# Attention and mixture-of-experts block in fp32: where the softmax is divided by its sums

## The chip, the cores and the metric

The kernel runs on one core of one Trainium2 chip. The metric is the device time of one execution in microseconds (us). Engines are named as in the profile: PE is TensorE, PEld its weight loads, DVE is VectorE, ACT is ScalarE, POOL is GpSimd, SP is SyncE, whose queue issues most of the transfers.

## The reference, cut

64 blocks of 128 tokens: `x` is 64 x 128 x 256, the context 64 x 128 x 192. First a cross attention with 4 heads of 64, the keys being the 128 context rows and the block's own 128 rows:

```
xn, ln = layernorm(ctx), layernorm(layernorm(x))
q = ln @ Wq.T;  k, v = concat([xn @ Wkv.T, ln @ Wlkv.T])      # 256 keys
attn = softmax(where(mask, rmsnorm(q) * SCALE @ rmsnorm(k).T, -max))   # over the 256 keys
out = attn @ v                                                # by head
x = x + out @ Wo.T + bo
```

Then each token's normalised row goes to the 4 best of 32 experts (grouped top-k routing, gated feed-forward of width 128) and through a shared gated feed-forward of width 256; both are added to `x`. The change touches only `softmax` and `attn @ v`.

## The kernel before

All is fp32. The first stage, up to about 700 us, is attention and routing. It works through 32 units of two blocks each; a `Unit` `u` has blocks j = 0 and 1, and b = 2 * u.n + j counts blocks. The stage is software pipelined by hand: `in_order(step, UNITS)` runs `step(s)` for s = 0 to 31 on every engine, and each engine's `step` is a fixed order of calls that concern several units at a time: the attention of unit s, the projections of the next unit `a = s + 1`, the router of `cc = s - 2`, the slot assignment of `r = s - 3`, the input statistics of `run = s + 3` and `ahead = s + 4`. An engine runs its list strictly in that order, and semaphores (`wait_ge`, `then_inc`) join the lists. So the order of calls within a step decides what waits behind what. Steps 3 to 30 have all of these parts; steps 0 to 2 lack the router or the assignment, and step 31 has no next unit.

The attention of one block j of unit s goes as follows.

- PE `scores(s, j)` writes 4 heads x 128 queries x 256 keys into PSUM (`psS` for j = 0, `psT` for j = 1), line 813, with the mask, line 818.
- DVE `maxima(s, j)`, line 1460, takes the row maxima.
- ACT `exps(s, j)`, line 1160, writes `probs` in SBUF, one head at a time, and the row sums `den` (128 x 4).
- DVE `invert_sums(s, j)`, line 1466, makes `rden = 1 / den`, 128 x 4.
- ACT `weigh_probs(s, j)`, line 1168, multiplies the 4 heads of `probs`, 128 x 256 each, by `rden` in place.
- PE `turn_probs(s, j)`, line 827, transposes them in 8 pieces; ACT `probs_copy(s, j)`, line 1175, brings them back to SBUF.
- PE `mix_values(s, j)`, line 840, 16 matmuls into `psO[:, 0:256]`: the outputs come out turned, 64 rows of a head by 128 queries. ACT `o_copy(s, j)`, line 1182, copies them to `oT`.
- PE `out_proj(s, j)`, line 852; DVE `residual`, line 1473, adds the result to `x1`.

For the next unit DVE does `square_sums(a, j)` (line 1418), `norms` (a chain of small operations that ends at line 1448), `scale_heads(a, j)` (line 1454); then PE turns keys and queries (`turn_k`, lines 791 and 792, `turn_q`, line 800) and ACT copies them (`k_copy`, line 1200, `q_copy`, line 1206). `scores` of the next step needs `q_copy`. In DVE's step the router's operations follow: `best_groups`, then `best_experts` and `choose_experts` (from line 1506).

DVE's order within a full step: `maxima(s,0)`, reading the ranks and assigning, `invert_sums(s,0)`, `maxima(s,1)`, rest of the assignment and `top_scores(cc)`, `invert_sums(s,1)`, `square_sums` twice, `norms`, `scale_heads` twice, `best_groups`, `best_experts`, `choose_experts`.

PE's order: `scores(s,0)`, turning and positions for the router, `scores(s,1)`, logits, the projections of `a` (lines 757, 767, 770), `turn_probs(s,0)`, `project_v` (line 778) twice, `turn_c`, `mix_values(s,0)`, `turn_x`, `turn_probs(s,1)`, `out_proj(s,0)`, `turn_k(a,0)`, `mix_values(s,1)`, `turn_k(a,1)`, `turn_q(a)`, `out_proj(s,1)`.

After the attention come the first part of the shared feed-forward, the expert tiles (about 749 to 1190 us), and the rest of the shared part with the sums. POOL scatters the routed rows during the attention stage, paced by PE's semaphores.

Of the kernel before, what the change touches and what calls it, by code (L numbers as in the profile page):

```python
# [17 lines left out]
P = 128  # L18
NB, D, DC = 64, 256, 192
H, DH = 4, 64  # L20
# [66 lines left out]
def build(nc, x, ctx, mask, gains, w_in_lat, w_in_ctx, wo, bo,  # L87
# [8 lines left out]
    with ExitStack() as c:  # L96
# [45 lines left out]
        probsT = part(2, 2, H * P)  # L142
        oT = part(D)
        vv = part(4 * 2, H, DH)

# [27 lines left out]
        nmax = sb("nmax", [P, 2, H])  # L173
        den, rden = sb("den", [P, 2, H]), sb("rden", [P, 2, H])

# [63 lines left out]
        s_full, m_done, exp_done = sem("s_full"), sem("m_done"), sem("exp_done")  # L239
        den_done, rden_done = sem("den_done"), sem("rden_done")  # L240
        spread = [sem("spread0"), sem("spread1")]
        pt_full, pt_ev = sem("pt_full"), sem("pt_ev")
        pv_full, ot_ev = sem("pv_full"), sem("ot_ev")
        y_full, y_done = sem("y_full"), sem("y_done")
# [465 lines left out]
        def _(pe):  # L710
# [111 lines left out]
            def turn_probs(u, j):  # L822
# [6 lines left out]
                m.then_inc(pt_full, 1)  # L829

            def mix_values(u, j):
                b = 2 * u.n + j
                pe.wait_ge(pt_ev, b + 1)
                pe.wait_ge(pc_free, 2 * u.n + 2)
                ge(pe, ot_ev, b)
                for ch in range(2):
                    for key in range(2):
                        for r in range(2):
                            g, h = 2 * r + ch, 2 * ch + r
                            m = pe.matmul(psO[r * DH:(r + 1) * DH, ch * P:(ch + 1) * P],  # L840
                                          vv[:, 4 * u.par + 2 * j + key, h, :], probsT[:, j, key, g * P:(g + 1) * P],
                                          start=key == 0, stop=key == 1)
                m.then_inc(pv_full, 1)
# [87 lines left out]
            def step(s):  # L931
# [12 lines left out]
                if a.exists():  # L944
                    project_q(a, 0)
                    project_kv(a)
                    project_q(a, 1)
                turn_probs(s, 0)
                if a.exists():
                    project_v(a, 0)  # L950
                    project_v(a, 1)
# [5 lines left out]
                turn_probs(s, 1)  # L957
                out_proj(s, 0)
                if a.exists():
                    turn_k(a, 0)  # L960
# [121 lines left out]
        def _(act):  # L1082
# [72 lines left out]
            def exps(u, j):  # L1155
                b = 2 * u.n + j
                act.wait_ge(m_done, b + 1)
                ge(act, pt_full, b - 1)
                for g in range(H):
                    a = act.activation(probs[:, j, g, :], score_banks[j][:, g // 2, g % 2], ACT.Exp,  # L1160
                                       bias=nmax[:, j, g:g + 1], accum_out=den[:, j, g:g + 1])
                a.then_inc(den_done, 1)

            def weigh_probs(u, j):
                b = 2 * u.n + j
                act.wait_ge(rden_done, b + 1)
                for g in range(H):
                    a = act.activation(probs[:, j, g, :], probs[:, j, g, :], ACT.Copy, scale=rden[:, j, g:g + 1])  # L1168
                a.then_inc(exp_done, 1)
# [7 lines left out]

            def o_copy(u, j):
                b = 2 * u.n + j
                act.wait_ge(pv_full, b + 1)  # L1180
                ge(act, y_full, b)
                act.activation(oT, psO[:, 0:D], ACT.Copy).then_inc(ot_ev, 1)

# [25 lines left out]
            def step(s):  # L1209
# [9 lines left out]
                if cc.exists():  # L1219
                    logit_exp(cc)  # L1220
                weigh_probs(s, 0)
                if a.exists():
                    projected_q(a, 0)
                exps(s, 1)
                if a.exists():
                    projected_kv(a, 0)
                    projected_kv(a, 1)
                    projected_q(a, 1)
                probs_copy(s, 0)
                if a.exists():  # L1230
                    values_copy(a, 0)
                    values_copy(a, 1)
                weigh_probs(s, 1)
                o_copy(s, 0)
                if (s + 2).exists():
                    inputs_x(s + 2)
                probs_copy(s, 1)
                if (s + 2).exists():
                    inputs_c(s + 2)
                if a.exists():  # L1240
                    k_copy(a, 0)
                o_copy(s, 1)
                if a.exists():
# [120 lines left out]
        def _(dve):  # L1364
# [98 lines left out]
            def invert_sums(u, j):  # L1463
                b = 2 * u.n + j
                dve.wait_ge(den_done, b + 1)
                dve.reciprocal(rden[:, j, :], den[:, j, :]).then_inc(rden_done, 1)  # L1466

# [180 lines left out]
            def step(s):  # L1648
# [30 lines left out]

                def between_choices(n):  # L1680
                    if ahead.exists() and G_LINKS < n <= G_LINKS + 4:
                        input_part(ahead, n - G_LINKS - 1)
# [19 lines left out]
                if a.exists():  # L1702
                    square_sums(a, 0)
                    square_sums(a, 1)
                norms(run, between_roots if a.exists() else None)
                if a.exists():
                    scale_heads(a, 0)
                    scale_heads(a, 1)
                    if r.exists():
                        give_slots(r)  # L1710
# [4 lines left out]
                if not cc.exists() or not a.exists():  # L1715
                    residual(s, 0)
                    x1_statistics(s, 0)
                if not cc.exists():
                    if ahead.exists():
                        input_statistics(ahead)  # L1720
# [248 lines left out]
```

## Time and profile before

| | before |
|---|---|
| runs | 1341.43, 1343.05, 1344.83 us (median 1343.05) |
| profiled execution | 1343.46 us, its span 1341.5 us |
| granted TensorE clock, mean | 0.985 |
| busy share of the span | PE 97%, PEld 78%, DVE 72%, ACT 75%, POOL 48% |
| busy in 45 to 700 us (655 us) | PE 641.7, DVE 566.8, ACT 614.9, POOL 329.1 us |
| busy in 780 to 1110 us (330 us) | PE 330.0, DVE 177.9, ACT 230.1, POOL 210.1 us |

The second part of the table reads per stage: in the attention stage three engines are over 85% busy, in the expert stage only PE is full. The span is what the profiler saw from the first to the last instruction; the execution's own time is 1.96 us longer.

### The profile page before, as it was taken

Reading aid. Unit: us, or ns where it says so; the run is one execution under the profiler, and the core shown is the slowest. Engines: PE = TensorE matmul, PEld = TensorE weight load, DVE = VectorE, ACT = ScalarE, POOL = GpSimd, SP = SyncE. Lnnn points to the kernel's source line nnn. Section 1 sums busy time; section 2 is a strip of 40 time slices with the busy share of each in tenths; the row PEclk is TensorE's granted clock in tenths of the full one; section 3 lists DMA queues with packets and bytes.
Section 4 is the critical chain, followed back from the end, with each engine's and each line's share of the span. In section 5 each row is a group of like instructions: output and inputs, shape, how many; then the busy total and the mean of one; then the engine's idle time right before and its main releaser. Section 6 shows DMA issues by size and latency. Waiting matters only on the chain.

```text
span 1341.5 us, 32944 instructions
## 1 busy us (share of the span) xinstructions
PE 1298.0 (97%) x8718; PEld 1043.2 (78%) x8718; DVE 972.0 (72%) x4498; ACT 1011.6 (75%) x2730; POOL 643.4 (48%) x724
## 2 busy tenths in 40 slices
PE   6999999999999999999979899999999999999997
PEld 4566676676676766766658799999999999988886
DVE  4578898888988988888887455555555555548887
ACT  4899999999999999999851566766776676653332
POOL 1113555555555555555455366666666666640000
PEclk8999999999999999999989899999999999999999
DMA  8234645535545445454487655555655555438896
GB/s 278 84 133 136 205 162 176 192 131 187 176 138 190 161 153 195 136 179 162 168 304 246 194 169 172 172 172 168 178 169 174 169 173 166 132 114 313 304 319 218
DMA packets 147714, 247.14 MB, mean 184 GB/s; under 512 B 24139, under 2 KB 110413, under 8 KB 146896
## 3 DMA queue, kind: packets, MB, share of 16 engines
q1 hardware_dynamic: 121472, 177.63, 41.3%
q0 software_dynamic: 26064, 67.42, 14.5%
q8 instruction: 77, 1.26, 0.4%
q14 instruction: 101, 0.83, 0.2%
HBM read 104.68 MB, written 119.96 MB: 167 GB/s over the span
## 4 chain that ended last, share of the span: by engine, by line
PE 63%; ACT 21%; DVE 9%; issue 5%; DMA 2%; SPq 0%; POOL 0%; ACTq 0%; DVEq 0%
PE psT L1033 10%; PE ps L1033 9%; PE psS L1043 9%; ACT arena L1168 6%; PE ps L916 6%; PE ps L1024 5%; PE ps L852 4%; ACT arena L1160 4%; PE psS L927 3%; PE psT L827 3%; PE psS L813 3%; PE psO L840 2%; ACT arena L1128 2%; ACT arena L1132 2%; ACT arena L1175 2%
## 5 line engine op out<-in xcount | busy, mean ns | idle before, releaser
L701 POOL DMA_INDIRECT expert_out<-pay,dest x287 | 282.1, 983 | 175.1 <-DVE dest L1878 157.4
L556 POOL DMA_INDIRECT lists<-pay,slot x168 | 174.3, 1037 | 187.7 <-PE psT L827 39.6
L1043 PE MATMUL psS<-arena,history 128*128 x574 | 171.8, 381 | 0.3 <-DVE history L1865 0.3
L1033 PEld LDWEIGHTS ps<-pad,hist_j 128*128 128x128 f32 x1152 | 152.1, 193 | 9.5 <-ACT pad L1315 2.1
L1033 PEld LDWEIGHTS psT<-pad 128*128 128x128 f32 x1144 | 151.0, 192 | 7.3
L1033 PE MATMUL ps<-pad,hist_j 128*128 128x128 f32 x1152 | 152.8, 276 | 1.9 <-ACT pad L1315 1.9
L1033 PE MATMUL psT<-pad 128*128 128x128 f32 x1144 | 151.6, 276 | 0.0
L1872 DVE TENSOR_SCALAR pay<-psS,dest 128x256 f32<-128x256 f32 x287 | 138.9, 484 | 1.6 <-PE psS L1043 1.5
L757 PE MATMUL ps<-arena 128*128 128x512 f32 x256 | 128.3, 624 | 2.6 <-ACT arena L1120 2.0
L556 POOL DMA_INDIRECT lists<-arena,slot x88 | 91.0, 1034 | 79.4 <-PE psT L827 20.6
L1168 ACT ACTIVATE arena<-arena,rden 128x256 f32<-128x256 f32 x256 | 109.1, 503 | 15.2 <-DVE rden L1466 15.1
L1865 DVE TENSOR_TENSOR history<-history,psT 128x128 f32<-128x128 f32 x143 | 41.2, 288 | 102.4 <-ACT history L1326 102.4
L1865 DVE TENSOR_TENSOR history<-history,ps 128x128 f32<-128x128 f32 x144 | 41.5, 288 | 101.2 <-ACT history L1326 101.2
L1024 PE MATMUL ps<-ident,pay 128*128 128x128 f32 x574 | 110.0, 274 | 3.1 <-DMA arena<-in_gate_up 3.0
L1315 ACT ACTIVATE pad<-ps 128x256 f32<-128x256 f32 x287 | 107.7, 375 | 0.0
L1320 ACT ACTIVATE hist_j<-arena 128x512 f32 x144 | 89.6, 622 | 9.4 <-issue 7.6
L1326 ACT ACTIVATE history<-ps 128x128 f32<-128x128 f32 x144 | 39.9, 277 | 70.3 <-PE ps L1033 70.3
L757 PEld LDWEIGHTS ps<-arena 128*128 128x128 f32 x256 | 44.2, 193 | 59.2 <-issue 59.2
L1320 ACT ACTIVATE pad<-arena 128x512 f32 x143 | 88.8, 621 | 0.0
L1326 ACT ACTIVATE history<-psT 128x128 f32<-128x128 f32 x143 | 39.7, 278 | 65.0 <-PE psT L1033 65.0
L1043 PEld LDWEIGHTS psS<-arena,history 128*128 128x128 f32 x574 | 86.9, 192 | 0.7 <-issue 0.7
L1418 DVE TENSOR_REDUCE va<-arena 128x12 f32<-128x768 f32 x64 | 61.0, 953 | 34.2 <-ACT arena L1128 29.1
(238 smaller groups left out, 3284.1 us busy)
## 6 DMA issues: line engine op xcount, KB each, us to landing
lists<-pad SPq DMA_DIRECT2D x72, 516.0 KB, 5.2
pay<-lists SPq DMA_DIRECT2D x287, 129.0 KB, 2.2
arena<-expert_out SPq DMA_DIRECT2D x32, 1024.0 KB, 7.1
pay<-pay SPq DMA_DIRECT2D x42, 384.0 KB, 3.6
x<-in_x SPq DMA_DIRECT2D x32, 256.0 KB, 4.7
out<-arena SPq DMA_DIRECT2D x31, 256.0 KB, 5.8
arena<-arena SPq DMA_DIRECT2D x20, 384.0 KB, 3.4
arena<-in_ctx SPq DMA_DIRECT2D x32, 192.0 KB, 4.6
```

The lines of the kernel that those rows point to most:

```text
L556: pool.indirect_dma_start(lists, bass.IndirectOffsetOnAxis(ap=slots(u)[:, j, k:k + 1], axis=0), paid(u)[:, j, k, :], None).then_inc(scat[3 ...
L701: pool.indirect_dma_start(expert_out, bass.IndirectOffsetOnAxis(ap=dest[:, t % DESTS, 1:2], axis=0), yy[n], None, bounds_check=T * TOPK - ...
L757: m = pe.matmul(ps[0][:, :], lnT[:, k, tok], w_lat[:, k, 0:2 * D], start=k == 0, stop=k == 1)
L916: m = pe.matmul(up_banks[u % 2][mm][:, which * D:(which + 1) * D], w[:, k, mm * P:(mm + 1) * P], n1T_of(u)[:, k, :], start=k == 0, stop=k ...
L1024: m = pe.transpose(ps[n % 2][:, k * P:(k + 1) * P], xs[n][:, k * P:(k + 1) * P], ident[:, :])
L1033: m = pe.matmul(ps[2 + n % 2][:, which * P:(which + 1) * P], w_now[1 - n % 2][:, k, which * I:(which + 1) * I], xsT[:, n % 2, k * P:(k + 1 ...
L1043: pe.matmul(dbank[n % 2][:, 0:D], hh[:, n % 4, :], w_dn[:, at(e, 1), :].rearrange("p a n -> p (a n)"), start=True, stop=True)\
L1168: a = act.activation(probs[:, j, g, :], probs[:, j, g, :], ACT.Copy, scale=rden[:, j, g:g + 1])
L1315: act.activation(xsT[:, n % 2, :], ps[n % 2][:, 0:D], ACT.Copy).then_inc(xst_ev, 1)
L1320: act.activation(w_now[1 - n % 2], w_gu[:, at(e, 1)].rearrange("p a k n -> p (a k) n"), ACT.Copy)\
L1865: dve.tensor_tensor(hh[:, n % 4, :], sg[:, n % 4, :], ps[2 + n % 2][:, P:2 * P], ALU.mult)\
L1872: dve.tensor_scalar(yy[n], dbank[n % 2][:, 0:D], dest[:, t % DESTS, 0:1].bitcast(fp32), None, ALU.mult)\
```

## The change

`exps` now signals `exp_done` itself, and `turn_probs` turns the undivided exponentials. `invert_sums` writes the inverse sums wide, 128 x 256: each head's inverse 64 times side by side, in the order of the output rows. PE's new `turn_sums` transposes this in two 128 x 128 pieces into `psO[:, 256:512]`, ACT's `sums_copy` (in place of `o_copy`) brings it to SBUF as `wide_sums`, and DVE's new `divide` multiplies `psO[:, 0:256]` by it into `oT`. `weigh_probs` and `o_copy` are gone. `divide(s, 0)` stands on DVE after `norms`, `divide(s, 1)` in the middle of `best_experts`.

```diff
--- before.py
+++ after.py
@@ -141,6 +141,8 @@
         probs = part(2, H, 2 * P)
         probsT = part(2, 2, H * P)
         oT = part(D)
+        wide_sums = part(D)
+        rden = part(2, D)
         vv = part(4 * 2, H, DH)
 
         pay_mid = part(2, TOPK, ROW)
@@ -171,7 +173,7 @@
         va, ra, nb = sb("va", [P, 30]), sb("ra", [P, 30]), sb("nb", [P, 6])
         ry, rt = sb("ry", [P, 30]), sb("rt", [P, 30])
         nmax = sb("nmax", [P, 2, H])
-        den, rden = sb("den", [P, 2, H]), sb("rden", [P, 2, H])
+        den = sb("den", [P, 2, H])
 
         esc = sb("esc", [P, 2, E])
         sc = sb("sc", [P, 2, E])
@@ -237,9 +239,10 @@
         pa_free, pb_free, pc_free = sem("pa_free"), sem("pb_free"), sem("pc_free")
         sq_full, ss_done, scaled = sem("sq_full"), sem("ss_done"), [sem("scaled0"), sem("scaled1")]
         s_full, m_done, exp_done = sem("s_full"), sem("m_done"), sem("exp_done")
-        den_done, rden_done = sem("den_done"), sem("rden_done")
+        rden_done = sem("rden_done")
         spread = [sem("spread0"), sem("spread1")]
         pt_full, pt_ev = sem("pt_full"), sem("pt_ev")
+        sums_turned, sums_ev = sem("sums_turned"), sem("sums_ev")
         pv_full, ot_ev = sem("pv_full"), sem("ot_ev")
         y_full, y_done = sem("y_full"), sem("y_done")
         pay_x, lg_full, lg_exp = sem("pay_x"), sem("lg_full"), sem("lg_exp")
@@ -828,11 +831,19 @@
                                          probs[:, j, g, key * P:(key + 1) * P], ident[:, :])
                 m.then_inc(pt_full, 1)
 
+            def turn_sums(u, j):
+                b = 2 * u.n + j
+                pe.wait_ge(rden_done, b + 1)
+                ge(pe, ot_ev, b)
+                for ch in range(2):
+                    m = pe.transpose(psO[:, D + ch * P:D + (ch + 1) * P], rden[:, j, ch * P:(ch + 1) * P], ident[:, :])
+                m.then_inc(sums_turned, 1)
+
             def mix_values(u, j):
                 b = 2 * u.n + j
                 pe.wait_ge(pt_ev, b + 1)
                 pe.wait_ge(pc_free, 2 * u.n + 2)
-                ge(pe, ot_ev, b)
+                pe.wait_ge(sums_ev, b + 1)
                 for ch in range(2):
                     for key in range(2):
                         for r in range(2):
@@ -946,6 +957,7 @@
                     project_kv(a)
                     project_q(a, 1)
                 turn_probs(s, 0)
+                turn_sums(s, 0)
                 if a.exists():
                     project_v(a, 0)
                     project_v(a, 1)
@@ -956,6 +968,7 @@
                     turn_x(s + 2)
                 turn_probs(s, 1)
                 out_proj(s, 0)
+                turn_sums(s, 1)
                 if a.exists():
                     turn_k(a, 0)
                 mix_values(s, 1)
@@ -1156,16 +1169,10 @@
                 b = 2 * u.n + j
                 act.wait_ge(m_done, b + 1)
                 ge(act, pt_full, b - 1)
+                ge(act, rden_done, b - 1)
                 for g in range(H):
                     a = act.activation(probs[:, j, g, :], score_banks[j][:, g // 2, g % 2], ACT.Exp,
                                        bias=nmax[:, j, g:g + 1], accum_out=den[:, j, g:g + 1])
-                a.then_inc(den_done, 1)
-
-            def weigh_probs(u, j):
-                b = 2 * u.n + j
-                act.wait_ge(rden_done, b + 1)
-                for g in range(H):
-                    a = act.activation(probs[:, j, g, :], probs[:, j, g, :], ACT.Copy, scale=rden[:, j, g:g + 1])
                 a.then_inc(exp_done, 1)
 
             def probs_copy(u, j):
@@ -1175,11 +1182,11 @@
                 act.activation(probsT[:, j].rearrange("p k n -> p (k n)"),
                                score_banks[j][:, :, :, :].rearrange("p k a n -> p (k a n)"), ACT.Copy).then_inc(pt_ev, 1)
 
-            def o_copy(u, j):
+            def sums_copy(u, j):
                 b = 2 * u.n + j
-                act.wait_ge(pv_full, b + 1)
-                ge(act, y_full, b)
-                act.activation(oT, psO[:, 0:D], ACT.Copy).then_inc(ot_ev, 1)
+                act.wait_ge(sums_turned, b + 1)
+                ge(act, ot_ev, b)
+                act.activation(wide_sums, psO[:, D:2 * D], ACT.Copy).then_inc(sums_ev, 1)
 
             def n1_copy(u):
                 act.wait_ge(t_n, u.n + 1)
@@ -1218,7 +1225,6 @@
                 exps(s, 0)
                 if cc.exists():
                     logit_exp(cc)
-                weigh_probs(s, 0)
                 if a.exists():
                     projected_q(a, 0)
                 exps(s, 1)
@@ -1227,19 +1233,18 @@
                     projected_kv(a, 1)
                     projected_q(a, 1)
                 probs_copy(s, 0)
+                sums_copy(s, 0)
                 if a.exists():
                     values_copy(a, 0)
                     values_copy(a, 1)
-                weigh_probs(s, 1)
-                o_copy(s, 0)
                 if (s + 2).exists():
                     inputs_x(s + 2)
                 probs_copy(s, 1)
+                sums_copy(s, 1)
                 if (s + 2).exists():
                     inputs_c(s + 2)
                 if a.exists():
                     k_copy(a, 0)
-                o_copy(s, 1)
                 if a.exists():
                     k_copy(a, 1)
                     q_copy(a)
@@ -1462,8 +1467,18 @@
 
             def invert_sums(u, j):
                 b = 2 * u.n + j
-                dve.wait_ge(den_done, b + 1)
-                dve.reciprocal(rden[:, j, :], den[:, j, :]).then_inc(rden_done, 1)
+                dve.wait_ge(exp_done, b + 1)
+                ge(dve, sums_turned, b - 1)
+                dve.reciprocal(rden[:, j, :].rearrange("p (c r d) -> p c r d", c=2, r=2),
+                               den[:, j, :].rearrange("p (r c o) -> p c r o", c=2, o=1).to_broadcast([P, 2, 2, DH]))\
+                   .then_inc(rden_done, 1)
+
+            def divide(u, j):
+                b = 2 * u.n + j
+                dve.wait_ge(pv_full, b + 1)
+                dve.wait_ge(sums_ev, b + 1)
+                ge(dve, y_full, b)
+                dve.tensor_tensor(oT, psO[:, 0:D], wide_sums, ALU.mult).then_inc(ot_ev, 1)
 
             def residual(u, j):
                 b = 2 * u.n + j
@@ -1678,6 +1693,8 @@
                         x1_statistics(s, 0)
 
                 def between_choices(n):
+                    if n == G_LINKS + 1:
+                        divide(s, 1)
                     if ahead.exists() and G_LINKS < n <= G_LINKS + 4:
                         input_part(ahead, n - G_LINKS - 1)
 
@@ -1703,6 +1720,7 @@
                     square_sums(a, 0)
                     square_sums(a, 1)
                 norms(run, between_roots if a.exists() else None)
+                divide(s, 0)
                 if a.exists():
                     scale_heads(a, 0)
                     scale_heads(a, 1)
@@ -1716,6 +1734,7 @@
                     residual(s, 0)
                     x1_statistics(s, 0)
                 if not cc.exists():
+                    divide(s, 1)
                     if ahead.exists():
                         input_statistics(ahead)
 
```

## Rows read from the trace of the kernel before

**Rows 1.** Windows view, one step: start:end, length, busy PE, PEld, DVE, ACT, POOL; clock, DMA.
```profile
320.78:341.37 20.59, 20.46 (x138) 13.94 (x139) 18.36 (x106) 19.90 (x55) 11.27 (x13) 1.00 0.50 167
```

**Rows 2.** Starts of `maxima(s, 0)`, VectorE: start, us, engine, line, form, idle before.
```profile
94.30 1.22 DVE L1460 TENSOR_REDUCE nmax<-psS 128x4 f32<-128x1024 f32 x1 [0.60 <-PE psS L818]
...
320.78 1.23 DVE L1460 TENSOR_REDUCE nmax<-psS 128x4 f32<-128x1024 f32 x1 [0.52 <-PE psS L818]
...
341.37 1.22 DVE L1460 TENSOR_REDUCE nmax<-psS 128x4 f32<-128x1024 f32 x1 [0.53 <-PE psS L818]
...
670.77 1.22 DVE L1460 TENSOR_REDUCE nmax<-psS 128x4 f32<-128x1024 f32 x1 [1.25 <-PE psS L818]
```

**Rows 3.** The same step on VectorE in order of time.
```profile
324.40 0.18 DVE L1466 RECIPROCAL rden<-den 128x4 f32<-128x4 f32 x1
...
329.20 0.18 DVE L1466 RECIPROCAL rden<-den 128x4 f32<-128x4 f32 x1 [0.40 <-ACT arena L1160]
...
331.26 0.95 DVE L1418 TENSOR_REDUCE va<-arena 128x12 f32<-128x768 f32 x1 [0.90 <-ACT arena L1128]
...
334.99 1.83 DVE L1454 TENSOR_TENSOR arena<-arena,ra 128x768 f32<-128x768 f32 x2
...
338.29 0.29 DVE L1506 TENSOR_TENSOR t<-sfc,gm 128x32 f32<-128x32 f32 x2
```

**Rows 4.** VectorE costs by line (min/median/max ns), and one group of the lines view.
```profile
L1480 DVE RECIPROCAL sc<-esc x32: 543/544/553, 78.9 to 703.6; 128x64 f32<-128x64 f32 x32
...
L1553 DVE RECIPROCAL wsum<-wsum x31: 165/166/167, 96.9 to 716.5; 128x2 f32<-128x2 f32 x31
...
L1473 DVE TENSOR_TENSOR x<-x,ps x64: 395/414/422, 49.1 to 691.7; 128x256 f32<-128x256 f32 x64
...
L1570 DVE TENSOR_TENSOR code<-code,later 128x64 f32<-128x64 f32 x27 | 6.1, 225 | 0.9
```

**Rows 5.** The same step on ScalarE in order of time.
```profile
324.61 1.70 ACT L1168 ACTIVATE arena<-arena,rden 128x256 f32<-128x256 f32 x4 [0.53 <-DVE rden L1466]
...
333.06 1.69 ACT L1168 ACTIVATE arena<-arena,rden 128x256 f32<-128x256 f32 x4
...
338.36 0.41 ACT L1182 ACTIVATE arena<-psO 128x256 f32<-128x256 f32 x1
...
338.86 0.60 ACT L1200 ACTIVATE arena<-ps 128x512 f32<-128x512 f32 x1
...
339.35 0.68 ACT L1206 ACTIVATE arena<-ps,gain 128x512 f32<-128x512 f32 x1
```

**Rows 6.** The same step on TensorE in order of time.
```profile
335.74 1.03 PE L852 MATMUL ps<-arena 128*128 128x256 f32 x4
...
336.61 0.27 PE L791 MATMUL ps<-ident,arena 128*128 128x128 f32 x1
...
337.14 1.09 PE L840 MATMUL psO<-arena 128*64 128x128 f32 x16
...
338.16 0.33 PE L791 MATMUL ps<-ident,arena 128*128 128x128 f32 x1
...
338.65 0.62 PE L800 MATMUL ps<-ident,arena 128*128 128x128 f32 x4
...
340.08 1.13 PE L813 MATMUL psS<-arena 64*128 64x256 f32 x8
```

**Rows 7.** Waits of TensorE weight loads in 100 to 650 us: sum, times, longest.
```profile
PEld psT L827 <- ACT arena L1168: 9.9, 27, 0.4
...
PEld psS L813 <- ACT arena L1206: 9.4, 27, 0.4
```

**Rows 8.** TensorE clock before the last step: windows, then two timeline rows.
```profile
670.00:673.00 3.00, 0.73 (x8) 0.30 (x5) 1.22 (x1) 0.83 (x2) 1.93 (x2) 1.00 0.40 155
...
676.00:680.00 4.00, 4.00 (x17) 3.36 (x14) 3.75 (x20) 2.20 (x8) 0.97 (x1) 0.50 1.13 388
...
674.06 2.08 PE L813 MATMUL psT<-arena 64*128 64x256 f32 x8
```

## The prediction

> **What bounds the kernel now.** I read the page first, then the windows view to see which stage the change touches. It touches the attention stage alone, the first 700 us. There one step is a cycle of 20.59 us in which PE is busy for 20.46, ACT for 19.90 and DVE for 18.36 [rows 1]. The starts of `maxima(s, 0)` give the step more exactly: from step 3 to step 31 they go from 94.30 to 670.77 us, 28 steps of 20.59 us [rows 2]. All else was read from the timeline of one of them, the one from 320.78 to 341.37.
>
> PE and ACT are both nearly full. DVE, which gets the new work, looks like the one with room, and its room is what the argument turns on. It waits visibly three times in a step: 0.53 us for the scores [rows 2], 0.40 us for the second sums and 0.90 us for a projected square [rows 3]. That is 1.83 us. The other 20.59 - 1.83 = 18.76 us are work and the small gaps between dependent operations, and they stay.
>
> **The change part by part.** *ACT loses `weigh_probs`.* Two groups of four take 1.70 and 1.69 us, and the wait of 0.53 us for the inverse in front of the first goes too [rows 5]. `sums_copy` costs what `o_copy` cost, the same 128x256 from the same PSUM tile, 0.41 us. So ACT's step falls by 3.4 us of work to about 16.5 us busy. Time comes of this only if ACT was what the step waits for and nothing else takes its place.
>
> *PE gains `turn_sums`*, two 128x128 transposes for each block, four in a step. The four of `turn_k(a, 1)` take 338.65 - 338.16 = 0.49 us [rows 6], so PE needs at most 20.46 + 0.49 = 20.95 us. Of that up to 0.7 us is a wait for ACT that the busy row can hide: 9.9 and 9.4 us over 27 steps in front of the second `turn_probs` and of `scores` [rows 7]. PE thus wants between 20.2 and 20.95 us: as much as the step now has.
>
> *DVE's `invert_sums` goes from 4 to 256 elements a row.* This is the price that decides, and the trace has no reciprocal of this size. It has three smaller ones: 2 elements 166 ns, 4 elements 180 ns [rows 3, 4], 64 elements 544 ns [rows 4]. From 4 to 64 that is 6.1 ns an element, against 1.0 ns for a plain tensor operation (225 ns for 64 elements, 414 ns for 256) [rows 4]. A reciprocal is thus paid by the element. Estimate: 180 + 252 x 6.1 = 1717 ns, 1.54 us more than now, twice a step: 3.08 us. Bounds: from below, all beyond 64 elements at the plain rate, 544 + 192 x 1.0 = 740 ns, that is 2 x 0.56 us; from above, everything proportional, 4 x 544 = 2180 ns, 2 x 2.0 us. I take 1.72 us, since the small ones show a fixed part (2 elements cost as much as 92% of 4) and a slope that no plain operation has.
>
> The Trainium skill ("VectorE: DVE Perf Modes", First, the fixed hardware budget) says that the reciprocal is an iterative divide with a repeat count of 8 on an engine of 0.96 GHz. If that count is taken as cycles per element it is 8.3 ns, an estimate of 2.13 us for 256 elements; it would put the sum below near the upper bound. The rows give 6.1 ns, so they agree on the kind of cost and not on its size.
>
> *DVE gains `divide`*, twice a step. The nearest row is `residual`, a 128x256 tensor operation of SBUF and PSUM, 0.41 us [rows 4]. Operations overlap by some 0.08 us at their ends, so 0.33 us each, 0.66 us in a step.
>
> *The sum on DVE*: 18.76 + 3.08 + 0.66 = 22.50 us, against a step of 20.59. DVE's 1.83 us of waiting are spent and 1.91 us are missing. DVE becomes the engine that sets the step.
>
> *The new waits.* `divide(s, 0)` stands behind `norms`, and PE holds `out_proj(s, 0)`, `turn_sums(s, 1)`, `turn_k(a, 0)`, `mix_values(s, 1)`, `turn_k(a, 1)` and `turn_q` in line behind it. So the second limit is a loop. `norms` ends and `scale_heads` begins now 14.21 us after `maxima(s, 0)` [rows 2, 3]; without the waits of 0.40 and 0.90 us and with both reciprocals that is 12.91 + 3.08 = 15.99 us. `divide` lands at 16.40. `out_proj` starts at about 16.5 and takes 336.61 - 335.74 = 0.87 us; `turn_sums` lands 0.38 us later, at 17.75; `sums_copy` 0.41 us, to 18.16; `mix_values` from 18.26 takes 338.16 - 337.14 = 1.02 us; `turn_k` 0.49 us, to 19.77; `turn_q` lands 0.62 us later [rows 5, 6], at 20.39. ACT can begin `q_copy` then, `k_copy` being 0.49 us ahead of it; from the start of `q_copy` to the next `maxima` it is 341.37 - 339.35 = 2.02 us [rows 2, 5]. The loop closes at 22.4 us. It lies 0.1 us under DVE's own sum, so the two limits will now and then hold each other up, and I take 22.6 us. `divide(s, 1)` comes due on DVE at about 19.7 (338.29 is 3.30 us behind the start of `scale_heads` [rows 3]), when `mix_values(s, 1)` has just landed; it holds `out_proj(s, 1)`, which PE reaches at 20.3, so it costs nothing more.
>
> The moved signals cost nothing: the exponentials of a block are ready before DVE comes to invert their sums (0.40 us late now in the second case, early after, as DVE itself comes 1.5 us later), and `turn_probs` stands behind projections that PE has to do first. POOL's scatters and SP's transfers follow PE's semaphores, POOL is busy 11.27 of 20.59 us [rows 1], and a longer step gives them room.
>
> *The total*: 28 full steps x (22.6 - 20.59) = 56 us. Steps 0 to 2 lack the router's share of DVE's work and hide the new work. The last step and the way out of the stage get one reciprocal and one `divide` on their path, 1.54 + 0.41 = 2 us. 1343.46 + 58 = 1402 us for an execution like the profiled one, which lies 0.4 us over the median of the runs; I say 1402.
>
> **The rivals.** *The reciprocal is dearer than its slope*: at 2.18 us DVE's sum is 23.4 and the loop 23.3 us, so 23.5 for the step, 28 x 2.9 + 2.5 = 84 us, 1427 us. The 8-fold repeat would do about this. Against it: 64 elements at 8.3 ns would leave 0.01 us for all else in an operation of 0.544 us, and 2 elements already take 0.166 us [rows 4].
>
> *The wait at `out_proj(s, 0)` is longer than drawn*, by ACT's fixed order (`sums_copy(s, 1)` behind `probs_copy(s, 1)`) or landings that I put too short. One microsecond more in the loop gives 23.4 us a step, 1425 us. For it: the loop has some seven hand-overs from one engine to another. Against it: ACT is 6 us idle in such a step.
>
> *TensorE's clock falls.* Ahead of the last step PE did 0.73 us of work in 3 us, and then ran at granted clock 0.50, 1.2 GHz instead of 2.4; eight score matmuls took 2.08 us [rows 8], against 1.13 us at full clock [rows 6]. If the new gap in front of `out_proj(s, 0)`, about 1.5 us, did this in each step, some 2.5 us would go each time, on the loop: 1402 + 70 = 1472 us. Against it: PE still is busy some 20.5 of 22.6 us.
>
> *No difference*: the wide reciprocal costs only its extra elements at the plain rate, 0.74 us. DVE's sum is 18.76 + 1.12 + 0.66 = 20.54 us, PE sets the step at 20.6 to 20.7, 1343 to 1347 us.
>
> *Faster*: ACT was holding PE. With ACT 3.4 us lighter PE's waits of 0.7 us go, PE gains 0.49, and the step is 20.59 - 0.7 + 0.49 = 20.38 us: 28 x 0.21 = 6 us, 1337 us. It needs a sum on DVE no longer than that: 18.76 + 0.66 + two increments of at most 0.48, so a wide reciprocal of at most 0.18 + 0.48 = 0.66 us, hardly above the 0.544 us that a quarter of it takes. From that point on the added work decides.
>
> **How the numbers follow.** The likeliest, 1.72 us for the reciprocal with DVE's sum as the limit: 0.75, with a range of its own of 1390 to 1418 (step 22.2 to 23.2). Dearer reciprocal 0.07, longer loop 0.06, clock 0.04, no difference 0.04, faster 0.04. The range reaches down past the likeliest by a few microseconds for a cheaper reciprocal and up to the first two rivals, 1385 to 1430. A measurement of this kernel tells 0.3%, 4 us, from nothing: faster 0.04, same 0.04, slower 0.92.
>
> **What would show it.** In the timeline after: RECIPROCAL 128x256 at about 1.7 us; starts of `maxima(s, 0)` 22.6 us apart; DVE busy for over 21.5 us of a step and its waits for ACT gone; ACT idle for 5 to 6 us, PE waiting for DVE ahead of `out_proj(s, 0)`, at an unchanged clock; the stages after 700 us moved as a block. The prediction is wrong if the reciprocal comes under 0.8 us, or if PE's wait at `out_proj(s, 0)` spreads to more than about 2 us.

## The result and the profile after

The changed kernel takes 1403.6 us in the median of 4 runs (1402.6 to 1404.5) against 1343.9 us for the kernel before; the ratio is 1.0445, 95% interval 1.0424 to 1.0465. The profiled execution took 1403.49 us with a span of 1401.5 us, at the same mean granted clock of 0.985.

The windows view over one step of the changed kernel, to be held against [rows 1] (start:end, length, busy PE, PEld, DVE, ACT, POOL, clock, DMA share, GB/s):

```profile
323.38:345.95 22.57, 21.05 (x142) 14.46 (x143) 21.98 (x108) 17.01 (x48) 11.59 (x13) 1.00 0.45 152
```

DVE went from 18.36 to 21.98 us busy and is the fullest engine; ACT fell from 19.90 to 17.01; PE rose from 20.46 to 21.05 at full clock. The starts of `maxima(s, 0)`, as in [rows 2], for steps 3, 4 and 31 (timeline of DVE):

```profile
97.84 1.23 DVE L1465 TENSOR_REDUCE nmax<-psS 128x4 f32<-128x1024 f32 x1 [0.37 <-PE psS L821]
120.26 1.23 DVE L1465 TENSOR_REDUCE nmax<-psS 128x4 f32<-128x1024 f32 x1
...
729.06 1.22 DVE L1465 TENSOR_REDUCE nmax<-psS 128x4 f32<-128x1024 f32 x1 [0.93 <-PE psS L821]
```

28 steps take 631.22 us, 22.54 each, against 20.59. That is 54.7 us of the 60.0 by which the span grew. The row at 120.26 has no bracket any more: the view names no idle time of DVE ahead of it. The rest: from `maxima(31, 0)` to the end 672.4 us instead of 670.7, 1.7 us; steps 0 to 2 together 61.68 instead of 60.80 us, 0.9 us; and the first `maxima` comes at 36.16 instead of 33.50 us, 2.7 us.

The new and changed groups of DVE (lines view, 100 to 650 us: count, then busy us and mean ns, then idle before), and the step on DVE and PE in order of time (timeline views):

```profile
L1472 DVE RECIPROCAL arena<-den 128x256 f32<-128x256 f32 x50 | 87.7, 1753 | 1.7
...
L1481 DVE TENSOR_TENSOR arena<-psO,arena 128x256 f32<-128x256 f32 x48 | 20.2, 421 | 0.8
```

```profile
332.96 1.75 DVE L1472 RECIPROCAL arena<-den 128x256 f32<-128x256 f32 x1
...
339.28 0.42 DVE L1481 TENSOR_TENSOR arena<-psO,arena 128x256 f32<-128x256 f32 x1
...
343.13 0.42 DVE L1481 TENSOR_TENSOR arena<-psO,arena 128x256 f32<-128x256 f32 x1
...
345.63 0.17 DVE L1543 TENSOR_TENSOR before<-before,chosen 128x32 bf16<-128x32 bf16 x1
```

```profile
333.44 0.38 PE L839 MATMUL psO<-ident,arena 128*128 128x128 f32 x2
...
339.76 1.13 PE L863 MATMUL ps<-arena 128*128 128x256 f32 x4 [1.40 <-DVE arena L1481]
...
341.28 0.27 PE L795 MATMUL ps<-ident,arena 128*128 128x128 f32 x1
341.68 1.09 PE L851 MATMUL psO<-arena 128*64 128x128 f32 x16
...
345.63 0.28 PE L821 MATMUL psS<-mask_row,ones_sq 64*128 64x256 bf16 x2
```

The divisions start 15.90 and 19.75 us behind `maxima(s, 0)` at 323.38; the prediction had 15.99 and 19.7. PE stands 1.40 us ahead of `out_proj(s, 0)` (line 863) until `divide(s, 0)` is done, and a smaller hold is seen between the last turned key at 341.28 and `mix_values(s, 1)` at 341.68, which waits for the copy of the turned sums.

The last row of each view shows how the step closes. By the ends that the profile gives, DVE's last operation ends at 345.63 + 0.17 = 345.80 us, PE's last mask matmul of the next scores at 345.63 + 0.28 = 345.91, and the next `maxima(s, 0)` starts at 345.95. So DVE does wait, for 0.14 us, too short for the view to name; nearly every full step has this gap, 0.13 to 0.15 us. DVE's own work, with the small gaps inside it, takes 22.43 us of the step, and the loop through PE closes last by 0.14 us.

### The profile page after: what moved, and what is told of

It reads as the page before. It is cut to its first block, busy times and chain, and to the rows that moved or that the text cites. A ratio compares the mean times of both kernels' runs of the same rounds, so it can differ in the third digit from the quotient of the medians.

```text
span 1401.5 us, 33170 instructions
## 1 busy us (share of the span) xinstructions
PE 1316.2 (94%) x8846; PEld 1060.6 (76%) x8846; DVE 1086.0 (77%) x4562; ACT 918.8 (66%) x2474; POOL 650.1 (46%) x724
## 4 chain that ended last, share of the span: by engine, by line
PE 59%; DVE 30%; issue 7%; ACT 2%; DMA 1%; SPq 0%; ACTq 0%; DVEq 0%; POOL 0%
PE ps L1046 9%; PE psT L1046 9%; PE psS L1056 9%; PE ps L927 5%; PE ps L863 5%; PE ps L1037 4%; DVE nmax L1465 4%; DVE arena L1472 4%; DVE va L1423 3%; PE psS L938 3%; PE psO L851 3%; DVE arena L1604 3%; PE psS L816 3%; PE psT L927 2%; PE ps L794 1%
## 5 line engine op out<-in xcount | busy, mean ns | idle before, releaser
L559 POOL DMA_INDIRECT lists<-pay,slot x168 | 166.3, 990 | 213.6 <-PE ps L773 32.6
L559 POOL DMA_INDIRECT lists<-arena,slot x88 | 87.0, 989 | 102.5 <-PE psT L830 16.6
L1472 DVE RECIPROCAL arena<-den 128x256 f32<-128x256 f32 x64 | 112.2, 1753 | 9.7 <-ACT arena L1174 7.7
L863 PE MATMUL ps<-arena 128*128 128x256 f32 x256 | 70.8, 400 | 42.5 <-DVE arena L1481 42.4
L549 POOL TENSOR_TENSOR x<-x,bo_b 128x512 f32<-128x512 f32 x32 | 40.7, 1273 | 95.2 <-PE psS L821 95.2
```

The lines of the kernel that those rows point to most:

```text
L559: pool.indirect_dma_start(lists, bass.IndirectOffsetOnAxis(ap=slots(u)[:, j, k:k + 1], axis=0), paid(u)[:, j, k, :], None).then_inc(scat[3 ...
L863: m = pe.matmul(ps[1][:, 0:D], oT[:, k * P:(k + 1) * P], w_o[:, k, :], start=k == 0, stop=k == 1)
L1472: dve.reciprocal(rden[:, j, :].rearrange("p (c r d) -> p c r d", c=2, r=2), den[:, j, :].rearrange("p (r c o) -> p c r o", c=2, o=1).to_br ...
```

## The experiments

The theory: DVE's own work sets the step, mostly by the wide reciprocal (A). The rival: the new hand-overs through `divide`, the turned sums and their copies set it, whatever DVE's load (B). A third question came up on the way: what PE's four new transposes (0.44 us a step) cost, and what ACT's relief is worth.

| kernel | time, before beside it (us) | ratio, 95% interval | step (us) |
|---|---|---|---|
| before | 1343.9 | 1 | 20.59 |
| changed | 1403.6 | 1.0445 (1.0424 to 1.0465) | 22.54 |
| e1, spare wide reciprocal | 1377.6 / 1344.3 | 1.0252 (1.0235 to 1.0269) | 21.78 |
| e2, narrow, PE widens | 1380.0 / 1344.3 | 1.0258 (1.0240 to 1.0276) | 21.80 |
| e3, narrow, ACT widens | 1380.4 / 1344.3 | 1.0264 (1.0247 to 1.0282) | 21.68 |
| e4, divide late | 1490.2 / 1344.3 | 1.1078 (1.1058 to 1.1098) | 25.46 |
| e5, divide early | 1405.6 / 1343.8 | 1.0457 (1.0439 to 1.0476) | 22.55 |
| e6, no weighing | 1331.6 / 1343.8 | 0.9912 (0.9894 to 0.9930) | 20.23 |
| e7, widened in ACT's gaps | 1357.4 / 1343.8 | 1.0101 (1.0083 to 1.0120) | 21.01 |
| e8, sums together | 1357.9 / 1343.8 | 1.0101 (1.0083 to 1.0119) | 21.02 |
| e9, spare turns | 1420.3 / 1406.7 | 1.0097 (1.0079 to 1.0115) | 21.15 |
| e10, copy for reciprocal | 1413.2 / 1406.7 | 1.0043 (1.0029 to 1.0057) | 20.98 |
| e11, divide first | 1416.3 / 1406.7 | 1.0085 (1.0067 to 1.0104) | 20.79 |
| e12, one block | 1350.7 / 1344.8 | 1.0037 (1.0022 to 1.0051) | 20.88 |

The step is the distance of the starts of `maxima(3, 0)` and `maxima(31, 0)` in each trace, over 28. In some traces this mean holds a few longer steps, whose cause was not looked for: most steps are 20.89 us in e7 and e10, 21.02 in e9 and 20.80 in e12.

Runs e9 to e11 were made on another chip, on which the kernel before took 1406.7 us; their times are read only as ratios to that. The extra 60 us lie behind the attention stage: from `maxima(31, 0)` to the end of the span it is 730 to 735 us in e9 to e11, against 671 in the kernel before. Their steps are compared with 20.59 us, though no trace shows the step of the kernel before on that chip. The traced execution of e10 took 1417.0 us and is the slowest of its five.

**e1: the reciprocal alone.** The kernel before with

```diff
                 dve.reciprocal(rden[:, j, :], den[:, j, :]).then_inc(rden_done, 1)
+                dve.reciprocal(spare[:, j, :].rearrange("p (c r d) -> p c r d", c=2, r=2),
+                               den[:, j, :].rearrange("p (r c o) -> p c r o", c=2, o=1).to_broadcast([P, 2, 2, DH]))
```

> The kernel before, with the wide reciprocal added on DVE behind the narrow one; nothing reads its result, and no other part of the change is made. Theory A (DVE's time is what the change costs): DVE's occupied 18.8 us of a step grow by 2 x 1.67 to 22.1, the step goes from 20.6 to 22.1 to 22.6, the time to 1387 to 1401. Rival B (the new hand-overs through divide, turned sums and their copy cost the time): nothing of them is here, so the step stays at 20.6 to 20.9 and the time at 1344 to 1352.

It took 1377.6 us, ratio 1.0252: more than half of the whole loss with none of the hand-overs. Its windows view of one step and the group of the reciprocal (lines view):

```profile
312.69:334.48 21.79, 20.68 (x138) 13.88 (x139) 21.38 (x109) 20.25 (x55) 11.00 (x13) 1.00 0.47 157
```

```profile
L1468 DVE RECIPROCAL arena<-den 128x256 f32<-128x256 f32 x52 | 89.5, 1722 | 0.0
```

DVE is busy for 21.38 of 21.79 us. The step is 0.3 us under the 22.1 of the expectation, so the 18.8 us that I had taken as fixed contained about 0.3 us that a fuller DVE does not need. Rival B gave at most 20.9 and falls as the sole cause. DVE's last operation ends here as the next `maxima` begins: the gap of 0.14 us is absent.

**e2 and e3: narrow sums.** The changed kernel with the narrow reciprocal, and the widening given to PE (e2) or to ACT, in two copies ahead of `probs_copy` (e3):

```diff
-                dve.reciprocal(rden[:, j, :].rearrange("p (c r d) -> p c r d", c=2, r=2),
-                               den[:, j, :].rearrange("p (r c o) -> p c r o", c=2, o=1).to_broadcast([P, 2, 2, DH]))\
-                   .then_inc(rden_done, 1)
+                dve.reciprocal(rden4[:, j, :], den[:, j, :]).then_inc(rden_done, 1)
...
+                    for r in range(2):                                            # e2, for each ch
+                        m = pe.matmul(psO[r * DH:(r + 1) * DH, D + ch * P:D + (ch + 1) * P],
+                                      rden4[:, j, 2 * r + ch:2 * r + ch + 1].to_broadcast([P, DH]), ident[:, :],
+                                      start=True, stop=True)
...
+                act.activation(rden[:, j, :].rearrange("p (c r d) -> p c r d", c=2, r=2),   # e3, widen(u, j)
+                               rden4[:, j, :].rearrange("p (r c o) -> p c r o", c=2, o=1).to_broadcast([P, 2, 2, DH]),
+                               ACT.Copy).then_inc(widened, 1)
```

> The changed kernel with the inverse sums kept narrow (128x4, 0.18 us); PE widens them while it turns them, by four 64-column matmuls on a repeated column per block. Theory A: DVE's occupied time falls to 19.2 to 19.5 us, PE is next with at most 20.9, the step is 20.4 to 20.9 and the time 1338 to 1352. Rival B: the hand-overs are all still here, so the step stays near 22 us and the time over 1385.

> The changed kernel with narrow inverse sums that ACT, which is idle for 5.5 us of a step, copies wide (two copies of some 0.4 us in a step). Theory A: DVE 19.2 to 19.5, PE at most 20.9, step 20.4 to 20.9, time 1338 to 1352. If ACT's order is what matters, one more copy ahead of probs_copy delays mix_values, and this is slower than the version where PE widens. Rival B: over 1385.

Both missed: 1380 us, a step of 21.8 and 21.7. With 3.1 us a step of reciprocals taken off DVE only 0.8 came back. The traces say why, each in its own way. In e2 (windows view of a step, then PE's widening matmuls in the timeline):

```profile
317.96:339.79 21.83, 21.83 (x154) 14.76 (x155) 19.03 (x107) 17.21 (x47) 11.25 (x13) 1.00 0.46 156
```

```profile
328.13 0.66 PE L839 MATMUL psO<-ident,rden 128*64 128x128 f32 x8
```

DVE is down to 19.03 us, and PE has no idle time at all in 21.83. My four matmuls are eight records, 328.13 to 328.72 us in the timeline, 0.6 us a block, where the two transposes of the changed kernel are two records, the next operation starting 0.22 us behind them: in the traces an fp32 matmul leaves two records and an fp32 transpose one. (The 16 matmuls of `mix_values` and the eight of `scores` named ahead of the result are records as well; the kernel issues 8 and 4.) The 0.38 us more for each block, twice a step, on top of PE's 21.0 us give the step of 21.8. In e3 PE waits instead (waits view, 100 to 650 us: sum, times, longest):

```profile
PE psO L840 <- ACT arena L1190: 15.1, 25, 0.6
```

That is 0.6 us a step at `turn_sums(s, 0)` for ACT's widening, which I had put too late in ACT's order.

**e4 and e5: the place of `divide(s, 0)`.** The same work, `divide(s, 0)` behind both `scale_heads` (e4), or in the middle of `norms` (e5):

```diff
-                divide(s, 0)
                 if a.exists():
                     scale_heads(a, 0)
                     scale_heads(a, 1)
+                divide(s, 0)                     # e4
...
+                    if n == 6:                   # e5, in between_roots
+                        divide(s, 0)
```

> The changed kernel with divide(s, 0) moved behind both scale_heads on DVE: the same work on every engine. If the loop over PE (out_proj, turned sums, copy, mix, turns of keys and queries, scores) is a limit as tight as DVE's sum, it grows by 1.74 us, the step to 24.3 and the time to 1452. If DVE's sum alone sets the step, it stays at 22.5 and the time at 1403.

> The changed kernel with divide(s, 0) moved forward on DVE, into the middle of norms (behind its sixth operation), some 1.5 us earlier; the same work on every engine. In the changed kernel the loop over PE and DVE's own sum close within 0.2 us of each other at 22.5 us. If DVE's sum is a limit of its own, taking 1.5 us out of the loop brings nothing: step 22.4 to 22.6, time 1399 to 1405. If the loop alone sets the step, it falls to PE's own need of 21.1 us, time 1365.

e5 took 1405.6 us, a step of 22.55: unchanged. In the timeline of DVE `divide(s, 0)` now stands at 14.53 us behind `maxima` instead of 15.90, and the next `maxima` again follows DVE's last operation by 0.14 us. PE's wait has gone from `out_proj(s, 0)` to `turn_k(a, 0)`, which waits for `scale_heads`, and 0.27 us of it to `out_proj(s, 1)`, which waits for `divide(s, 1)` (timeline of DVE, then of PE):

```profile
324.37 1.23 DVE L1465 TENSOR_REDUCE nmax<-psS 128x4 f32<-128x1024 f32 x1
...
338.90 0.42 DVE L1481 TENSOR_TENSOR arena<-psO,arena 128x256 f32<-128x256 f32 x1
...
346.95 1.22 DVE L1465 TENSOR_REDUCE nmax<-psS 128x4 f32<-128x1024 f32 x1
```

```profile
341.64 0.33 PE L794 MATMUL ps<-ident,arena 128*128 128x128 f32 x1 [0.91 <-DVE arena L1459]
344.61 1.13 PE L863 MATMUL ps<-arena 128*128 128x256 f32 x4 [0.27 <-DVE arena L1481]
```

So DVE's sum is a limit of its own: whatever is taken out of the loop, no more than 0.14 us a step can come back. e4 shows that the loop is one too, and dearer than I expected: 1490.2 us, a step of 25.46 instead of 24.3. Two rows of PE's timeline, from step 5 and from step 11, and two windows, the whole of step 5 and the gap in step 11, have the reason:

```profile
169.06 1.13 PE L863 MATMUL ps<-arena 128*128 128x256 f32 x4 [3.13 <-DVE arena L1481]
...
321.19 2.07 PE L863 MATMUL ps<-arena 128*128 128x256 f32 x4 [3.13 <-DVE arena L1481]
```

```profile
150.94:175.21 24.27, 21.01 (x142) 14.43 (x143) 22.16 (x107) 16.95 (x47) 11.22 (x13) 1.00 0.45 152
...
318.00:324.00 6.00, 2.87 (x10) 2.33 (x10) 3.88 (x20) 1.43 (x3) 2.68 (x3) 0.73 0.12 43
```

PE now stands for 3.0 to 3.1 us in front of `out_proj(s, 0)` in every step. In steps 3 to 5 the clock stays at 1.00, `out_proj` takes its 1.13 us, and the steps are 24.13, 24.27 and 24.27 us: the loop as I had counted it. From step 6 on they are about 25.6 us. Over the gap of step 11 the granted clock is 0.73, and the four records behind it take 2.07 us where they take 1.13 at full clock. So of what e4's later steps exceed those of the changed kernel by, 1.7 us are the loop, and the other 1.3 us come with the lower clock. This is the clock rival of the prediction, at 1.3 us a step and not 2.5. The same gap of 3.13 us leaves the clock full in three steps and goes with a fall in the later ones; what decides between them stays open. In the changed kernel, with its gap of 1.40 us, the clock is 1.00 in all 28 full steps.

**e6: what ACT's relief is worth.** The kernel before with `weigh_probs` and its signal removed (the probabilities stay undivided):

```diff
-                a.then_inc(den_done, 1)
-
-            def weigh_probs(u, j):
...
-                for g in range(H):
-                    a = act.activation(probs[:, j, g, :], probs[:, j, g, :], ACT.Copy, scale=rden[:, j, g:g + 1])
                 a.then_inc(exp_done, 1)
```

> The kernel before with weigh_probs left out and nothing in its place: the probabilities are never divided by their sums (this part of the computation is left out). ACT's step falls by 3.4 us. Theory A (PE is as full as ACT, so that the relief is worth only PE's waits for ACT, up to 0.7 us a step): step 20.0 to 20.4, time 1325 to 1338. Rival: ACT was the limit and its relief is worth most of what it loses: step under 19.5, time under 1313.

1331.6 us, 0.9912: the most that the idea could bring if the division were free is 12 us. ACT loses 3.4 us a step, and 0.36 of it arrive. Of the two waits of PE's weight loads for ACT in [rows 7], the one in front of `turn_probs(s, 1)`, 0.37 us a step, is gone; the one in front of `scores` is still 9.0 us over 27 steps, against 9.4, since `scores` waits for `q_copy` and with it for PE's own `turn_q`.

**e7 and e8: narrow sums, better placed.** e7 is e3 with the two widening copies in ACT's idle stretches. e8 also turns and copies the sums of both blocks together before `mix_values(s, 0)` and puts `divide(s, 0)` between the `scale_heads`.

```diff
-                widen(s, 0)
-                widen(s, 1)
                 probs_copy(s, 0)
...
                     logit_exp(cc)
+                widen(s, 0)
...
                     projected_kv(a, 1)
+                widen(s, 1)
```

> Narrow inverse sums that ACT copies wide, as in e3, but at the two places where ACT is idle (behind the first exponentials, and ahead of the last projection's square) and not in a row ahead of probs_copy. In e3 PE waited 0.6 us a step for the copy of the turned sums. If ACT's order was what e3 lost by, the step falls from 21.7 to 21.1, time 1362 to 1366; if not, it stays at 1378 to 1382.

> As e7, with the sums of both blocks turned together ahead of mix_values(s, 0), into the whole of psO, copied by one ACT copy of 512 columns, and with divide(s, 0) between the two scale_heads. This takes turn_sums and its copy out of the loop between divide(s, 0) and mix_values(s, 1). PE's added work is still 0.45 us a step. If the hand-overs are what held e2 and e3 near 21.8, the step falls to 20.6 to 21.0, time 1343 to 1355; if PE's added work with DVE's divide is what holds, it stays over 21.3, time over 1363.

e7 took 1357.4 us, a step of 21.01 instead of 21.68: ACT's order was what e3 lost by, and the time came out under the 1362 to 1366 us that I had expected. e8 took the hold at `mix_values` out and won nothing, 21.02; it stayed just over the range of its first branch, and a wait of PE's weight loads for `divide(s, 0)`, 0.3 us a step in front of `out_proj(s, 0)`, had come in place of the other.

**e9, e10, e11: the remaining parts singly.**

```diff
+            def spare_turns(u, j):               # e9, in the kernel before
+                ge(pe, ot_ev, 2 * u.n + j)
+                for ch in range(2):
+                    pe.transpose(psO[:, D + ch * P:D + (ch + 1) * P], ident[:, :], ident[:, :])
...
-                dve.reciprocal(rden[:, j, :].rearrange(...    # e10, in the changed kernel
+                dve.tensor_copy(rden[:, j, :].rearrange(...
```

> The kernel before with PE's new work alone: two transposes per block, of the identity into the unused half of psO, at the places of turn_sums; nothing reads them, nothing waits for them. They take 0.44 us of PE a step. If PE is full in the kernel before, the step grows by 0.35 to 0.45 us, to 20.95 to 21.05, time 1354 to 1357. If ACT held the step and PE's waits for ACT (0.7 us a step) absorb it, the step grows by at most 0.1 us, time 1343 to 1347.

> The changed kernel with one word changed: the wide reciprocal on DVE is a plain wide copy of the sums, same shapes, place and signals, so that outputs are multiplied by the sums instead of divided by them. If the reciprocal's price by the element is what puts the changed kernel at 22.5 us, DVE's sum falls by 2.8 us to 19.7 us and PE sets the step at 21.0 to 21.2, time 1357 to 1366. If writing 256 columns and the hand-overs cost the time whatever the operation, it stays over 1390.

> As e8, with divide(s, 0) back ahead of both scale_heads. In e8 PE waited 0.3 us a step for it at out_proj(s, 0). If PE's work alone is the limit then, the step falls from 21.02 to 20.7, time 1349 to 1352; if the other waits close up behind it, it stays at 1356 to 1359. Either way it says how far the idea gets when nothing but PE's and DVE's unavoidable work is left: over the kernel before, as long as PE's 0.44 us are added to an engine that is full.

e9: ratio 1.0097. Most steps are 21.02 us, 0.44 more than in the kernel before: PE's 0.44 us are paid in full, the kernel before has no room on PE for them. e10: ratio 1.0043, step 20.98. The wide copy in the reciprocal's place costs (lines view, 100 to 650 us):

```profile
L1472 DVE COPY arena<-den 128x256 f32<-128x256 f32 x53 | 15.9, 300 | 2.2 <-issue 0.4
```

300 ns against 1753 for the same shapes, and with that one word the step falls by 1.56 us. DVE loses 2.9 us; no more comes back because PE then sets the step. e7 has the same value on the chip of e1 to e8: its step is 1.54 us under that of the changed kernel. e11: step 20.79 and so the shortest of the versions that divide both blocks by the turned sums, but its ratio of 1.0085 is no better than that of e10, with runs from 1408 to 1421 us; I do not read more from it than that it does not reach the kernel before.

**e12: one block of two.** The kernel before, with block 0 alone divided by turned narrow sums and block 1 weighed by ACT:

```diff
-                weigh_probs(s, 0)
+                widen(s)
...
                 probs_copy(s, 0)
+                sums_copy(s)
...
-                o_copy(s, 0)
...
                 norms(run, between_roots if a.exists() else None)
+                divide(s)
```

> The kernel before with block 0 of each unit alone changed over to turned narrow sums (ACT widens, PE turns, ACT copies, DVE divides ahead of scale_heads); block 1 is weighed by ACT as before. ACT loses about 1.3 us a step, PE gains 0.22, DVE 0.3. The kernel without weighing has a step of 20.23 us, the kernel with both blocks changed and narrow sums 21.0. If PE's added work is paid in full and ACT's relief is worth 0.35 us as soon as PE no longer waits for it, the step is 20.4 to 20.6 us, ratio to the kernel before 0.994 to 1.000. If each hand-over costs about as much as half of the change of both blocks (0.4 us), it is 20.65 to 20.85, ratio 1.002 to 1.006.

Ratio 1.0037 (1.0022 to 1.0051), step 20.88, the mean lying just over the 20.85 of the second branch. Most steps are 20.80 us, and 20.59 and the 0.22 us of two transposes make 20.81. So the turns alone would account for the loss, with nothing left of ACT's relief; the run does not separate them from the other hand-overs. The half change is a small loss where the whole change with narrow sums is a larger one. No version that still divides by the sums beat the kernel before.

## Why the prediction was right

It gave 1402 us and the measurement is 1403.6, and the likeliest case is the one that happened. By its steps:

- *The wide reciprocal*, 1.72 us from a slope of 6.1 ns an element: 1.753 us in the changed kernel, 1.722 in e1. The upper bound of 2.18 and the 2.13 us worked out from the 8-fold repeat did not come. e10 shows what it costs with all else in place: at least 1.56 us of step, 44 us in 28 steps. That is less than the 2.9 us it adds to DVE, as PE sets the step without it.
- *`divide`*, 0.41 us: 0.42 us.
- *DVE's sum*, 22.50 us: it is 22.43 of a step of 22.57, and e5 shows that nothing is won by shortening only the loop. The part in it called fixed was 0.3 us too large by e1, and small items that I had not counted made up for most of it, so that the sum comes out this close is partly luck.
- *The loop.* `divide(s, 0)` predicted at 15.99 us behind `maxima`, found at 339.28 - 323.38 = 15.90; from there to the next `maxima` 6.42 us predicted, 345.95 - 339.28 = 6.67 found. That the two limits lie within 0.2 us of each other was right, though it is the loop that closes last, by 0.14 us, and not DVE. Steps 3 to 5 of e4 show that the loop binds as soon as it is longer.
- *PE*, between 20.2 and 20.95 us: it was 21.05. This was mis-sized. I had counted 0.7 us of waits for ACT as room that would open up. e6 shows that ACT's relief is worth 0.36 us, as only the wait at `turn_probs(s, 1)` goes, and e9 that the turns cost their full 0.44. The hand-overs add their own holds.
- *Clock*: the gap in front of `out_proj(s, 0)` was to be 1.5 us, it is 1.40, and the clock stayed at 1.00 in all 28 steps.
- *The ends*: the last step and the way out cost 1.7 us, against 2 predicted. Not predicted were 0.9 us in steps 0 to 2 and 2.7 us ahead of the first `maxima`. The latter begins before any changed instruction, and e10, which differs from the changed kernel in one operation, has its first `maxima` at 33.30 us; its cause stays open. By these 3.6 us the ends were mis-sized. They outweigh the 1.6 us that the steps came out shorter, 22.54 instead of 22.6, and the 0.3 us at the last step; that the total hits to 1.6 us is again partly luck.

What was wrong lies in the rivals. For "no difference" and "faster" I took a cheap reciprocal to be enough, with 0.66 us as the point from which it decides. e10 has a reciprocal's stand-in of 0.30 us and is still slower by 0.43%, e7 with 0.18 us by 1.0%. By the times PE's turns alone cost 13.5 us (e9) and ACT's relief alone brings 12.2 (e6). The two cancel within the intervals, and what the widening, the copies and `divide` cost comes on top: "faster" had nothing to win that a measurement would tell from noise.

The parts do not simply add. The reciprocal alone costs 33 us (e1), all the rest without it 6 us (e10, on the other chip), both together 60. Alone each is partly hidden by DVE's 1.83 us of waits; once the reciprocals have used them up, the two divisions are paid in full. Put on in this order, the loss of 54.7 us in 28 steps splits like this: ACT's relief -10 us (e6: 0.36 x 28), the turns, hand-overs, divisions and a wide operation at copy price +21 us (e10 against e6: 0.75 x 28), the reciprocal beyond the copy +44 us (changed against e10: 1.56 x 28). The last two use traces from different chips, so their border is good to a few microseconds at best.

## What to carry to other kernels

Where three engines are each over 85% busy, taking 3.4 us off one of them brought 0.36: price the receivers first, against their own room in a step, and the giver's relief last. A reciprocal is paid by the element here, 6.1 ns against 1.0 for a plain operation, so invert sums while they are narrow and widen them by a copy on an engine that waits anyway, at a place in its order where it waits. And a result that other engines queue behind has two prices, the engine's sum and the loop through the others; move it both ways to learn which binds.

## What the runs showed that I had not expected

An ordinary fp32 matmul leaves two records in PE's trace and an fp32 transpose one: four matmuls with 64 stationary columns took 0.6 us where two transposes of 128x128 took 0.22 (e2). And the clock: a standstill of 3.13 us in each step left it at 1.00 in steps 3 to 5 of e4 and went with a fall from step 6 on, to 0.73 over the 6 us around the gap, with the records behind it at about half speed. The 1.74 us of added delay cost 1.7 us of step while the clock was full and 3.0 us afterwards. The changed kernel's 1.40 us left it at 1.00 in all 28 steps.
